# Decoder on one core: weight rounding of the quantised stage moved into the combination, low-rank turnings moved ahead of the down projections

## The reference, cut to what matters

```python
def _act_fake_quant(x, clip_factor):
    scale = jax.nn.sigmoid(clip_factor) * jnp.max(jnp.abs(x)) / QMAX        # one scale for the tensor
    return jnp.clip(_ste_round(x / scale), -QMAX - 1.0, QMAX) * scale
def _weight_fake_quant(w):
    scale = jnp.max(jnp.abs(w), axis=1, keepdims=True) / QMAX               # one scale for each row
    return jnp.clip(_ste_round(w / scale), -QMAX - 1.0, QMAX) * scale
xq = _act_fake_quant(x, clip_x[0])
gate = jnp.einsum('bsh,ih->bsi', xq, _weight_fake_quant(w_gate))
up = jnp.einsum('bsh,ih->bsi', xq, _weight_fake_quant(w_up))
h = _act_fake_quant(jax.nn.silu(gate) * up, clip_down[0])
return jnp.einsum('bsi,hi->bsh', h, _weight_fake_quant(w_down))
```

## Time and profile before

| | |
|---|---|
| runs | 1591.47, 1602.62, 1606.71 us; median 1602.62 |
| profiled execution | 1600.73 us, its span 1598.8 us |
| busy share | TensorE 89%, VectorE 63%, ScalarE 51%, GpSimd 28% |
| mean granted TensorE clock | 0.924 of full |
| block of this case | about 1148 to 1218 us of the span |

### The profile page before, as it was taken

How to read it: one execution, slowest core, us unless ns; L and a number is a source line. 1 busy time by engine, 2 the same in 40 slices (tenths; PEclk the granted TensorE clock), 3 DMA queues, 4 the chain that set the end, 5 groups by cost and what they waited for, 6 DMA issues and landing times. The chain is left out here.

```text
span 1598.8 us, 30608 instructions
## 1 busy us (share of the span) xinstructions
PE 1428.9 (89%) x10825; PEld 700.1 (44%) x10849; DVE 1011.5 (63%) x2036; ACT 814.7 (51%) x1530; POOL 454.4 (28%) x654
## 2 busy tenths in 40 slices
PE   7988899999999999778987898999978799969987
PEld 5766533333454444336633452222335333523354
DVE  5776588888352221465557668999485677457746
ACT  4555547777533333304540056888654466446637
POOL 7122300000004566320036330111022355135511
PEclk8999999999999999889997798999976999899978
DMA  2000553120300000001000074221100531143100
GB/s 103 2 0 0 161 173 87 47 50 24 122 1 1 0 1 1 0 7 40 19 7 1 0 209 140 86 60 45 33 1 9 179 102 41 56 161 102 41 1 27
DMA packets 82519, 85.42 MB, mean 53 GB/s; under 512 B 7372, under 2 KB 68044, under 8 KB 81900
## 3 DMA queue, kind: packets, MB, share of 16 engines
q1 hardware_dynamic: 79160, 76.32, 15.6%
q10 hardware_dynamic: 3264, 7.87, 1.3%
HBM read 51.06 MB, written 32.51 MB: 52 GB/s over the span
## 5 line engine op out<-in xcount | busy, mean ns | idle before, releaser
L1469 ACT ACTIVATE arena<-ps 128x1024 f32<-128x1024 f32 x256 | 261.7, 1023 | 93.8 <-PE ps L1355 86.9
L1340 PE MATMUL ps<-k_stack,q_stack 49*128 49x512 bf16 x512 | 197.2, 391 | 11.4 <-DVE small L1487 6.7
L1355 PE MATMUL ps<-q_stack,k_stack 51*128 51x256 bf16 x1024 | 197.0, 277 | 0.5 <-ACT arena L1469 0.4
L1484 DVE CUSTOM_DVE_ANT_0 small<-ps,mask_b 128x512 bf16<-128x512 f32 x256 | 170.9, 689 | 32.0 <-PE ps L1340 29.2
L1487 DVE TENSOR_REDUCE small<-ps 128x1 f32<-128x512 f32 x256 | 164.5, 686 | 15.2 <-PE ps L1340 10.6
L1376 PE MATMUL ps<-arena,v_pad 128*32 128x256 f32 x2048 | 163.4, 393 | 1.1 <-ACT arena L1469 1.1
L1650 ACT ACTIVATE arena<-ps 128x384 f32<-128x384 f32 x256 | 117.9, 488 | 81.9 <-PE ps L1575 81.3
L1673 DVE TENSOR_REDUCE small<-ps 128x6 f32<-128x768 f32 x128 | 120.6, 955 | 54.3 <-PE ps L1553 53.3
L1133 POOL TENSOR_SCALAR_AFFINE_SELECT arena<-arena 128x256 f32<-128x256 f32 x256 | 102.3, 407 | 126.5 <-ACT arena L1650 126.1
L1253 POOL TENSOR_TENSOR small<-small 128x8 bf16<-128x8 f32 x64 | 12.8, 200 | 349.8 <-DVE small L1490 349.8
L2728 DVE TENSOR_TENSOR arena<-ps,arena 128x512 f32<-128x512 f32 x64 | 44.3, 692 | 102.2 <-PE ps L2645 102.1
(11 more groups left out here) (363 smaller groups left out, 2974.0 us busy)
## 6 DMA issues: line engine op xcount, KB each, us to landing
q_stack<-q_scratch SPq DMA_DIRECT2D x128, 96.0 KB
k_stack<-k_scratch SPq DMA_DIRECT2D x64, 192.0 KB
k_stack<-k_scratch SPq DMA_DIRECT2D x64, 96.0 KB
k_scratch<-arena SPq DMA_DIRECT2D x6, 768.0 KB, 3.9
arena<-in_ctxT SPq DMA_DIRECT2D x8, 512.0 KB, 6.3
k_scratch<-arena SPq DMA_DIRECT2D x14, 256.0 KB, 3.7
k_scratch<-arena SPq DMA_DIRECT2D x6, 512.0 KB, 4.8
arena<-in_ctxT SPq DMA_DIRECT2D x12, 256.0 KB, 3.0
```

The costliest lines, as they stand in the source:

```text
L1340: pe.matmul(ps[:, t, :], c.q_stack[par][64 * e:64 * e + ROW_MAX, pr, t * P:(t + 1) * P], c.k_stack[par][64 * e:64 * e + ROW_MAX, pr, :], s ...
L1355: mm = pe.matmul(ps[:, bank, (ch % 2) * S:(ch % 2 + 1) * S], c.k_stack[prv][64 * e:64 * e + ROWS, pr, ch * P:(ch + 1) * P], c.q_stack[prv] ...
L1469: act.activation(buf.probs[j % 8], ps[:, bank:bank + 2, :].rearrange("p a n -> p (a n)"), ACT.Exp, scale=scale).then_inc(g["probs"].sem, 1)
L1484: dve.tensor_tensor_reduce(buf.junk[t], ps[:, t, :], c.mask_b[:, M_X + t * SC:M_X + (t + 1) * SC], 1.0, FLOOR, op0=ALU.add, op1=ALU.max, a ...
```

## The change

The five VectorE instructions for the weights' scales go into `combine`, behind the reciprocal of the denominators, and the seven ScalarE roundings too, behind the copies of the numerators; both by the new argument `early`. TensorE turns all three weights at once behind the norm; ScalarE copies all three out, behind its two table loads. The filling matmuls are five in place of six. On TensorE each of the three low-rank turnings goes ahead of the down projection that it stood behind. GpSimd's instructions and all loads are as before.

```diff
@@ -1992,7 +1992,7 @@
     g[f"loaded{slot}"].advance(16)
-def combine(c, slot, norm, guard=False, gated=False):
+def combine(c, slot, norm, guard=False, gated=False, early=None):
@@ -2049,6 +2049,8 @@
         for t in TS:
             act.wait_ge(g["num"].sem, g["num"].at(t + 1))
             act.activation(num[:, t, :], ps[:, 1 + t % 2, :], ACT.Identity).then_inc(g["num_kept"].sem, 1)
+        if early:
+            early.scalar(act)
     def vector(dve):
         ready = g["num_gated" if gated else "num_kept"]
@@ -2066,6 +2068,8 @@
             dve.reciprocal(recip, recip).then_inc(g["den_recip"].sem, 1)
         else:
             dve.reciprocal(recip, ps[:, 0, 0:S]).then_inc(g["den_recip"].sem, 1)
+        if early:
+            early.vector(dve)
         for t in TS:
             dve.wait_ge(ready.sem, ready.at(t + 1))
             dve.wait_ge(g["den_spread"].sem, g["den_spread"].at(t + 1))
@@ -3047,16 +3051,44 @@
     def part(v, i):
         return v[:, i, :]
+    def turned_weights(i):
+        return ps[:, 4 + i, :].bitcast(BF16)[:, 0:QN * P]
+
     def sync(sp):
         sp.dma_start(w, c.io["w_quant"]).then_inc(g["weights_in"].sem, 16)
         sp.dma_start(clip, c.io["clips"]).then_inc(g["weights_in"].sem, 16)
         lora.load(sp)
+    def round_weights(act):
+        act.wait_ge(g["w_scaled"].sem, g["w_scaled"].at(1))
+        for i in range(2):
+            for a in range(QN):
+                s = slice(a * P, (a + 1) * P)
+                mm = act.activation(wr[:, i, s], w[:, i, s], ACT.Identity, scale=wrec[:, QN * i + a:QN * i + a + 1], bias=magic)
+            mm.then_inc(g["w_rounded"].sem, 1)
+        act.activation(part(wr, 2), part(w, 2), ACT.Identity, scale=wrec[:, 2 * NB:2 * NB + 1], bias=magic)\
+           .then_inc(g["w_rounded"].sem, 1)
+
+    def link(dve, mm):
+
+        made[0] += 1
+        mm.then_inc(g["quant_chain"].sem, 1)
+        dve.wait_ge(g["quant_chain"].sem, g["quant_chain"].at(made[0]))
+
+    def weight_scales(dve):
+        dve.wait_ge(g["weights_in"].sem, g["weights_in"].at(32))
+        for i in range(2):
+            dve.tensor_reduce(wmax[:, QN * i:QN * (i + 1)], part(w, i).rearrange("p (a n) -> p a n", a=QN), X, ALU.max,
+                              apply_absolute_value=True)
+        link(dve, dve.tensor_reduce(wmax[:, 2 * NB:2 * NB + 1], part(w, 2), X, ALU.max, apply_absolute_value=True))
+        link(dve, dve.tensor_scalar(wscale, wmax, 1.0 / 127, 1e-30, ALU.mult, ALU.max))
+        dve.reciprocal(wrec, wscale).then_inc(g["w_scaled"].sem, 1)
+
     def tensor(pe):
         def turn_weights_of(i):
             pe.wait_ge(g["w_quant"].sem, g["w_quant"].at(i + 1))
             for a in range(QN):
-                mm = pe.transpose(ps[:, 4 + i, :].bitcast(BF16)[:, a * P:(a + 1) * P], wq[:, i, a * P:(a + 1) * P],
+                mm = pe.transpose(turned_weights(i)[:, a * P:(a + 1) * P], wq[:, i, a * P:(a + 1) * P],
                                   c.ident_b[:, :])
             mm.then_inc(g["turned"].sem, 1)
@@ -3088,35 +3120,23 @@
             mm.then_inc(g["down"].sem, 1)
         norm_pe(norm, pe)
-        turn_weights_of(0)
-        turn_weights_of(1)
+        for i in range(3):
+            turn_weights_of(i)
         spread_max(0, 2)
-        turn_weights_of(2)
-        keep_clock(c, pe, 6, bank=0)
-        pe.wait_ge(g["weights_kept"].sem, g["weights_kept"].at(2))
+        keep_clock(c, pe, 5, bank=0)
+        pe.wait_ge(g["weights_kept"].sem, g["weights_kept"].at(3))
         for u in range(N):
             gate_up(u)
-        pe.wait_ge(g["w_down_kept"].sem, g["w_down_kept"].at(1))
         lora.turn_shift(pe, 6)
         pe.wait_ge(g["x_max"].sem, g["x_max"].at(3))
         pe.wait_ge(g["lora_kept"].sem, g["lora_kept"].at(2))
         pe.transpose(ps[:, 7, 0:P], amax[:, 2:3].to_broadcast([P, P]), c.ident[:, :]).then_inc(g["max_turned"].sem, 1)
         for t in range(NTI):
-            down(t)
             if t < NTI - 1:
                 lora.turn(pe, t, 4 + t)
+            down(t)
     def scalar(act):
-        def round_weights(i):
-            act.wait_ge(g["w_scaled"].sem, g["w_scaled"].at(1))
-            if i < 2:
-                for a in range(QN):
-                    s = slice(a * P, (a + 1) * P)
-                    mm = act.activation(wr[:, i, s], w[:, i, s], ACT.Identity, scale=wrec[:, QN * i + a:QN * i + a + 1], bias=magic)
-            else:
-                mm = act.activation(part(wr, 2), part(w, 2), ACT.Identity, scale=wrec[:, 2 * NB:2 * NB + 1], bias=magic)
-            mm.then_inc(g["w_rounded"].sem, 1)
-
         def round_x(t):
             act.activation(norm.tile(xr, t), norm.tile(c.xn, t), ACT.Identity, scale=rec[:, 0:1], bias=magic)\
                .then_inc(g["rounded"].sem, 1)
@@ -3125,23 +3145,19 @@
             act.wait_ge(g["gate"].sem, g["gate"].at(u + 1))
             act.activation(unit(h, u), ps[:, u % U, :], ACT.Silu, scale=up_scale[:, u % U:u % U + 1]).then_inc(g["silu"].sem, 1)
-        norm.preload(act)
-        for t in range(NTI):
-            norm.squares(act, t)
-            if t:
-                norm.deviation(act, t - 1)
-        round_weights(0)
-        norm.deviation(act, 3)
-        round_weights(1)
-        round_weights(2)
+        def keep_weights(i):
+            act.wait_ge(g["turned"].sem, g["turned"].at(i + 1))
+            act.activation(part(wT, i), turned_weights(i), ACT.Identity).then_inc(g["weights_kept"].sem, 1)
+
+        norm_act(norm, act)
         act.wait_ge(g["weights_in"].sem, g["weights_in"].at(32))
         act.activation(sig, clip, ACT.Sigmoid).then_inc(g["clip_sig"].sem, 1)
         act.activation(c.small[:, NT:NT + 1], c.consts[:, C_EPS:C_EPS + 1], ACT.Silu)
+        for i in range(3):
+            keep_weights(i)
         act.wait_ge(g["scaled"].sem, g["scaled"].at(1))
         round_x(0)
         round_x(1)
-        act.wait_ge(g["turned"].sem, g["turned"].at(3))
-        act.activation(part(wT, 2), ps[:, 6, :].bitcast(BF16)[:, 0:QN * P], ACT.Identity).then_inc(g["w_down_kept"].sem, 1)
         for u in range(N):
             if u in (0, U):
                 round_x(2 + u // U)
@@ -3154,28 +3170,12 @@
             lora.keep(act, n, 4 + n)
     def vector(dve):
-        def link(mm):
-
-            made[0] += 1
-            mm.then_inc(g["quant_chain"].sem, 1)
-            dve.wait_ge(g["quant_chain"].sem, g["quant_chain"].at(made[0]))
-
-        def weight_max(i):
-            if i < 2:
-                return dve.tensor_reduce(wmax[:, QN * i:QN * (i + 1)], part(w, i).rearrange("p (a n) -> p a n", a=QN), X, ALU.max,
-                                         apply_absolute_value=True)
-            return dve.tensor_reduce(wmax[:, 2 * NB:2 * NB + 1], part(w, 2), X, ALU.max, apply_absolute_value=True)
-
         def tensor_scale(i, n):
             dve.wait_ge(g["max_turned"].sem, g["max_turned"].at(i + 1))
-            link(dve.tensor_reduce(top[:, i:i + 1], ps[:, 7, 0:n * P], X, ALU.max))
-            link(dve.tensor_scalar(scale[:, i:i + 1], top[:, i:i + 1], sig[:, i:i + 1], 1.0 / 127, ALU.mult, ALU.mult))
+            link(dve, dve.tensor_reduce(top[:, i:i + 1], ps[:, 7, 0:n * P], X, ALU.max))
+            link(dve, dve.tensor_scalar(scale[:, i:i + 1], top[:, i:i + 1], sig[:, i:i + 1], 1.0 / 127, ALU.mult, ALU.mult))
             return dve.reciprocal(rec[:, i:i + 1], scale[:, i:i + 1])
-
-        def keep_weights(i):
-            dve.wait_ge(g["turned"].sem, g["turned"].at(i + 1))
-            dve.tensor_copy(part(wT, i), ps[:, 4 + i, :].bitcast(BF16)[:, 0:QN * P]).then_inc(g["weights_kept"].sem, 1)
         def lift_x(t):
@@ -3214,17 +3214,8 @@
             dve.scalar_tensor_tensor(xt, ps[:, t, :], down_scale, xt, ALU.mult, ALU.add).then_inc(g["residual"].sem, 1)
         lora.centre(dve)
-        for t in range(3):
-            norm.centre(dve, t)
-        dve.wait_ge(g["weights_in"].sem, g["weights_in"].at(32))
-        weight_max(0)
         norm.invert(dve, 0)
-        norm.centre(dve, 3)
         norm.invert(dve, 1)
-        weight_max(1)
-        link(weight_max(2))
-        link(dve.tensor_scalar(wscale, wmax, 1.0 / 127, 1e-30, ALU.mult, ALU.max))
-        dve.reciprocal(wrec, wscale).then_inc(g["w_scaled"].sem, 1)
         dve.wait_ge(g["ln_centred"].sem, g["ln_centred"].at(4))
         for t in range(NTI):
             if t < 2:
@@ -3235,12 +3226,10 @@
                 dve.tensor_reduce(amax[:, 0:1], norm.tile(c.xn, 0), X, ALU.max, apply_absolute_value=True).then_inc(g["x_max"].sem, 1)
         dve.wait_ge(g["ln_scaled"].sem, g["ln_scaled"].at(4))
         dve.tensor_reduce(amax[:, 1:2], c.xn[:, NT:], X, ALU.max, apply_absolute_value=True).then_inc(g["x_max"].sem, 1)
-        keep_weights(0)
-        keep_weights(1)
         dve.wait_ge(g["clip_sig"].sem, g["clip_sig"].at(1))
         tensor_scale(0, 2).then_inc(g["scaled"].sem, 1)
         dve.wait_ge(g["w_scaled"].sem, g["w_scaled"].at(1))
```

(14 more changed lines are left out.)

## The result

The changed kernel took 1583.32 us (median of six, 1575.75 to 1586.81), the kernel before 1600.86 in its six; the ratio is 0.989 (0.985 to 0.993). Later runs gave 0.994 (0.991 to 0.997) for the same pair. Over all runs of the two kernels for which a clock is on record the means are 1595.6 us for before (95 runs, standard error 0.5) and 1584.2 us for the changed kernel (20 runs, 1.1): 11.4 us faster. The six runs of before in the first comparison have no clock on record; with them its mean is 1595.9. Two executions in a slow state, one of before (1611.55 us) and one of a variant (6955.6 us), are left out of all means and ratios. The profiled execution took 1586.81 us, its span is 1584.9.

The account below looks back on a forecast made before the run. A chain passing between engines, none full, was taken to bound the block, so the last wait counts; 2.0 + 1.7 + 0.3 + 2.7 = 6.7 us gave 1595.9 from the median of 1602.62, taken as 1595, range 1586 to 1603.

Parts of the forecast that it names:

- The block's gain: Block from the combination through the quantised stage: four terms together make it 6.7 us shorter, bounds 3 to 8.5.
- Hidden work: Weight scales and roundings moved into the combination cost nothing, with 0.9 us to spare on VectorE and 0.5 on ScalarE.
- the slower rival: In the combination and norm, GpSimd holds every VectorE instruction it overlaps; net 2.8 us slower, 1605; net slower, chance 0.05.
- the delay of up to 0.6: Norm late by up to 0.6 us if GpSimd holds the low-rank weights' centring matrix on VectorE; taken as 0.
- late weights: Combination: a weight load landing over 7.6 us later than now would eat the gain; no chance given.
- Turned right behind the norm: TensorE turns the quantised weights without waiting for GpSimd, so the maximum of xn spreads 2.0 us sooner, bounds 1.5 to 2.3.
- GpSimd out of the way: First two xq steps on VectorE no longer held: 1.7 us; one filling matmul fewer may give 0.3 more.
- Turnings: Low-rank turnings ahead of the down projections, the first inside TensorE's 3.96 us wait: 2.7 us, bounds 2.0 to 4.2.
- The faster clock at the end: Rival: TensorE at 2.4 GHz in the down projections and turnings, 1.4 us more gain, total 8.1, 1594; chance 0.10.
- The turning was hidden: Down projections: the rival, an unhidden first turning, leaves only 4.0 us of gain, 1599; chance 0.10.
- the anchor: Whole kernel: base for the forecast, the median of three runs, 1602.62 us; those runs lie 15 us apart.
- a later stage at a lower clock: Behind the block: sign of being wrong, the stage gains but a later one runs slower-clocked; no size given.

Follow-up runs that it names:

- last turning back: Changed kernel with only the third low-rank turning put back between the third and last down projections; ratio 0.993 against the kernel before, block 63.78 us.
- seven fillings: Changed kernel with seven filling matmuls in place of five ahead of the gate projections; ratio 0.993 against the kernel before, block 63.57 us.
- the repeat: Both kernels run again without edits, twelve runs each; ratio 1.002 for the kernel before, 0.994 for the changed kernel.
- Fillings at the end: Changed kernel with seven filling matmuls before the gate projections and two unused matmuls behind the last down projection; ratio 0.997 against the kernel before.
- late dequantising: Changed kernel with GpSimd's dequantising of the low-rank weights made to wait for the scale of xn; block 64.85 us, one run.

## Why the prediction was wrong

Forecast were 1595 us, 1586 to 1603; measured were 1583.3, below the range. Point by point:

- **The block's gain: right.** The sum was 6.7 us; four profiles of each kernel give 69.7 - 63.05 = 6.7. The first pair alone gave 5.6, with TensorE's clock down earlier in that norm (0.90 from 1165 to 1169 us, 0.99 before; the reduction of xn starts 0.5 us later than I had it).
- **Hidden work: right.** Scales end 1.07 us ahead of the quotient (0.9 forecast), roundings 0.69 us ahead of the square (0.5), GpSimd runs 1157.3 to 1168.2 (1157.6 to 1168.4). No VectorE step of the combination grew beside it: the slower rival is out. The centring matrix at 1165.63 took 0.28 us as before, with GpSimd's third conversion 0.14 us from its end: the delay of up to 0.6 did not come. The maxima of the weights follow the reciprocal without a wait: late weights are out.
- **Turned right behind the norm: right**, 0.86 us from the transposes' release to VectorE where 0.81 was worked out, against 2.73 before: 1.9 us, forecast 2.0.
- **GpSimd out of the way: right in sum, wrong as a term of its own.** I wrote 1.7 us for the holds and 0.3 for the filling matmuls. One hold put back into the changed kernel cost its 1.16 us, but taking both away before was worth nothing: the first projection started 0.4 us behind them, and with the holds gone it did not move. The first product of gate and up came 4.1 us sooner in the block on the mean of four profiles (34.35 and 30.24), where I had 4.0. Without the turnings' move, holds and half of the fillings taken away together gave 1.3 us at the first projection and 0.9 in the block; the full sum needs all three. I had seen the 0.3 us and not said that it capped the 1.7.
- **Turnings: right.** The block's end, from the last maximum of h on, is 16.6 us in place of 19.15: 2.6 us, forecast 2.7. Alone they gave 2.5. The faster clock at the end did not come: it is 0.50 from 1197 to 1212 us. The turning was hidden: TensorE's wait fell from 3.96 to 1.37 us with it in front.
- **The step that failed first was the anchor.** I set the gain against the median of three runs, 1602.62, and took 1595. Ninety-five runs of the same kernel have a mean of 1595.6; the median of the three was 7 us high. The six runs of before in the first comparison, the three among them, were high too (1600.86), so this shows only in the later runs. The same 6.7 us against the mean would have been 1588.9. That is inside the range, but still 5 us over the changed kernel's mean of 1584.2.
- **The second was that I priced TensorE's clock only inside the block,** and so put the stages behind it at nothing. I wrote that a later stage at a lower clock would make me wrong; it was a later stage at a higher one. 11.4 us were measured where the block gives 6.7. A line fitted through the runs of both kernels, time against mean granted clock, gives 1.2 us for each 0.001 of clock, and at equal clock the changed kernel is 5.7 us faster (standard error 0.6), near the block's gain; the other 5.7 us go with a mean clock of 0.932 in place of 0.927. The split is rough: the same fit gives only 3.7 us (0.9) for the last turning back, whose block is 5.9 us shorter. That the rest goes with the clock is shown, by these runs and by the profiles, where behind the block only TensorE's time differs. Why the clock is higher is not: the end of the block has a part in the next stage and gives it back in the attention, and the low-rank stage's two levels, 2.7 us of the 6.8, stay open. Kernels whose block was no shorter came out between 0.997 and 1.002. But the extra gain is no luck of one set of runs: seven fillings and last turning back, on two other chips than the repeat, have means of 1583.5 and 1583.1 us, 12 to 13 below before's there, with blocks only 6 us shorter. Fillings at the end, with a block as short, has 1589.1, no more than its block gives. So it goes with the program, in a way that none of the theories tested here explains.

On the Trainium skill's rule (SBUF — State Buffer, Who interferes with whom): the experiment with late dequantising agrees that whoever begins second waits for the whole instruction, 1.45 in place of 0.29 us. The two-input case, which no row of the prediction showed, stands elsewhere in the trace of before. A VectorE product with both inputs in SBUF, then the next one of the same shape with GpSimd idle, and the GpSimd instruction that the first met:

```profile
838.07 3.37 DVE L1744 TENSOR_TENSOR arena<-arena 128x1024 f32<-128x1024 f32 x1
```

```profile
841.36 1.21 DVE L1744 TENSOR_TENSOR arena<-arena 128x1024 f32<-128x1024 f32 x1
```

```profile
837.51 2.85 POOL L1744 TENSOR_TENSOR arena<-arena 128x1024 f32<-128x1024 f32 x1 [17.43 <-ACT arena L1893]
```

The first took 3.37 us in place of 1.21 and ended 1.1 us behind GpSimd's: it was held until about the end of that instruction. So the caution about the centring matrix was justified; it met GpSimd by only 0.14 us and was not measurably held.

## What to carry to other kernels

Before a stall is given a price (here 1.7 us of holds, worth 0.0 by themselves), look what else ends within half a microsecond of it, unused filling work included: it caps the gain, and the terms can then only be taken together. Measure a small change by the length of its own block over several profiles, and anchor a forecast in us to more than three runs when these lie further apart than the gain. Work moved into idle time of two engines cost nothing here, and it was the third engine's queue, freed by it, that paid.

## What the runs showed of the hardware

- One stage of the same program differs by up to 6 us from run to run (the attention 124.6 to 130.4) with VectorE, ScalarE and GpSimd busy for the same time to 0.3 us; the granted clock of the stage goes with it (0.93 at 124.6, 0.88 at 129.5, 0.87 at 130.4).
- In all four profiles in which the next stage was at its shortest (24.2 us), the attention behind it was at its long level (130.2 to 130.6).
- GpSimd's product is held as well as VectorE: 1.72 us in place of 1.48 when VectorE's step ran as it began.
- VectorE instructions with one input in PSUM, and reductions, were not held beside GpSimd: the residual took 0.75 us, the mean's subtraction 0.69, the reduction of xn 1.75, each both with GpSimd busy and with it idle (profiles of before and after).
- A VectorE product of two SBUF inputs took 3.37 us beside a GpSimd product and 1.21 without one (before, 838 and 841 us).
